# Rotary attention on one core: where a key projection, the tiles of context sums and the placing of queries stand around the shared bank

## What is computed

```python
xn = layer_norm(x, gamma_x, beta_x)
ln = layer_norm(latents, gamma_l, beta_l)
q = (ln @ Wq).reshape(b, m, h, d)
kv_x = xn @ Wkv
kv_l = ln @ Wkv
...
k_x = rope_rotate_k(k_x)
...
sim = jnp.einsum('bhid,bhjd->bhij', q, k)
attn = jax.nn.softmax(sim, axis=-1)
out = jnp.einsum('bhij,bhjd->bhid', attn, v)
out = jnp.transpose(out, (0, 2, 1, 3)).reshape(b, m, INNER)
return out @ Wo
```

## Time and profile before

| what | value |
|---|---|
| median of 3 runs | 2913.48 us (2912.77 to 2924.5) |
| the profiled execution: its own time, its span | 2919.26 us, 2917.5 us |
| PE busy over the span | 2579.3 us, 88% |
| DVE, ACT, POOL busy over the span | 61%, 56%, 48% |
| the 64 steps of the stage | 1984.5 to 2706.6 us |

### The profile page before, as it was taken

One profiled execution on the slowest core, in us unless ns is written; L12 is line 12 of the kernel. 1 busy time (PEld: TensorE's weight loads), 2 busy tenths in 40 slices (PEclk: granted clock), 3 DMA queues, 4 the chain that ended last, 5 costly groups with the idle time before them and its releaser, 6 DMA issues. The chain is left out here.

```text
span 2917.5 us, 43850 instructions
## 1 busy us (share of the span) xinstructions
PE 2579.3 (88%) x16307; PEld 2153.6 (74%) x16307; DVE 1791.1 (61%) x3679; ACT 1629.2 (56%) x2848; POOL 1407.9 (48%) x1114
## 2 busy tenths in 40 slices
PE   5999998587999999999958695878999999999777
PEld 4899988376999999999957564775676676767546
DVE  7888874545555555555445445338888888888352
ACT  4888884334766666666623243325666666666322
POOL 1877774111766666666600260206566665664040
PEclk9999999788999999999978897888999999999875
DMA  3323321012010111111001240212000000000000
GB/s 108 100 73 104 104 58 36 14 30 86 24 46 24 41 29 37 33 35 35 12 7 43 71 113 16 59 22 62 17 24 13 24 20 17 24 13 1 25 1 15
DMA packets 222574, 117.83 MB, mean 40 GB/s; under 512 B 21368, under 2 KB 217632, under 8 KB 222368
## 3 DMA queue, kind: packets, MB, share of 16 engines
q1 hardware_dynamic: 222368, 115.11, 14.3%
HBM read 100.39 MB, written 13.64 MB: 39 GB/s over the span
## 5 line engine op out<-in xcount | busy, mean ns | idle before, releaser
L812 POOL TENSOR_TENSOR L_xattn_held<-L_xattn_held,L_xattn_shift 128x512 f32<-128x512 f32 (+1 forms) x613 | 763.0, 1289 | 298.4 <-ACT L_xattn_shift L732 298.4
L532 PEld LDWEIGHTS L_xattn_acc<-L_xattn_rows,L_xattn_held 128*128 128x128 f32 (+2 forms) x5120 | 619.7, 192 | 34.3 <-DVE L_xattn_mixed L915 8.7
L532 PE MATMUL L_xattn_acc<-L_xattn_rows,L_xattn_held 128*128 128x129 f32 (+2 forms) x5120 | 629.1, 276 | 5.2 <-DVE L_xattn_mixed L915 5.2
L936 DVE TENSOR_TENSOR L_xattn_running<-L_xattn_ring,L_xattn_running 128x512 f32<-128x512 f32 (+1 forms) x384 | 264.1, 688 | 270.3 <-PE L_xattn_ring L514 258.8
L1566 POOL TENSOR_TENSOR L_xattn_projected<-L_xattn_along,L_xattn_crossed 128x512 f32<-128x512 f32 (+1 forms) x256 | 271.9, 1073 | 280.8 <-DVE L_xattn_crossed L1633 278.7
L722 ACT ACTIVATE L_xattn_held<-L_xattn_held 128x512 f32<-128x512 f32 (+2 forms) x640 | 400.3, 631 | 0.2
L715 ACT COPY L_xattn_held<-L_xattn_ring 128x512 f32<-128x512 f32 (+1 forms) x416 | 243.3, 585 | 227.6 <-DVE L_xattn_running L936 193.1
L512 PE MATMUL L_xattn_ring<-L_xattn_queries_hi,L_xattn_keys_hi 128*128 128x512 f32 (+2 forms) x640 | 282.5, 441 | 3.4 <-DVE L_xattn_keys_lo L840 2.0
L514 PE MATMUL L_xattn_ring<-L_xattn_queries_hi,L_xattn_keys_lo 128*128 128x512 f32 (+2 forms) x640 | 254.4, 397 | 0.0
L513 PE MATMUL L_xattn_ring<-L_xattn_queries_lo,L_xattn_keys_hi 128*128 128x512 f32 (+2 forms) x640 | 253.8, 397 | 0.0
L1282 PE MATMUL L_xattn_sums<-L_xattn_probT,L_xattn_rows 128*128 128x256 f32 (+2 forms) x896 | 248.9, 385 | 0.6 <-ACT L_xattn_mixed L1458 0.6
(11 more groups left out here) (576 smaller groups left out, 4872.2 us busy)
## 6 DMA issues: line engine op xcount, KB each, us to landing
L_xattn_raw<-in_ctx SPq DMA_DIRECT2D x16, 768.0 KB
context_normalised<-L_xattn_fresh SPq DMA_DIRECT2D x16, 768.0 KB
L_xattn_rows<-context_normalised SPq DMA_DIRECT2D x16, 768.0 KB
L_xattn_fresh<-in_ctx SPq DMA_DIRECT2D x16, 768.0 KB
L_xattn_rows<-in_ctx SPq DMA_DIRECT2D x16, 768.0 KB
L_xattn_staged<-in_ctx SPq DMA_DIRECT2D x16, 768.0 KB
L_xattn_xhat<-context_normalised SPq DMA_DIRECT2D x16, 768.0 KB
L_ffn_w<-in_L_ffn_W SPq DMA_DIRECT2D x2, 896.0 KB, 5.3
```

The lines of the kernel that those rows point to most:

```text
L532: mm = nc.tensor.matmul(acc[:, c // 2, c % 2 * WIDE:(c % 2 + 1) * WIDE], held[0:n, u % 2, k, c * P:(c + 1) * P], rows[0:n, b % 2, k, :], s ...
L812: nc.gpsimd.tensor_tensor(tile, tile, shift[0:keys_of_tile[k]], ALU.subtract).then_inc(shifted, 1)
L936: seen = nc.vector.tensor_tensor(most, bank, most, ALU.max)
```

## The change

Three things move, and nothing is added or left out. On PE, in the quad that follows another use of `bank_a` (j - 1 in `BETWEEN[t]`), the projection of the chunk is issued ahead of the transposes instead of behind them. The tiles of sums are spread by a new table `SPLIT` (tiles ahead of the other use, tiles behind it): in steps 1 and 2, quad 1 keeps one on either side, and quad 2 has both ahead of the second transfer and none behind it. On ACT, `keep_queries` is cut in two: `take_queries` stays where it was, and `place_queries` with `keep_own` comes after the evacuation of the next quad.

```diff
@@ -1058,7 +1058,10 @@
-    PIECES = [[range(0, 2), range(2, 4), range(4, 6), range(6, 7)], [range(7, 9), range(9, 11), range(11, 13), range(13, KT)]]
+
+    HALF = KT // 2
+    SPLIT = {0: ((2, 0), (1, 1), (2, 0), (1, 0)), 1: ((2, 0), (1, 1), (2, 0), (1, 0)),
+             2: ((2, 0), (1, 1), (2, 0), (1, 0)), 3: ((2, 0), (2, 0), (1, 1), (1, 0))}
...
@@ -1268,20 +1271,20 @@
-            def sum_context(pair, parity, group, part, piece, turned, tiles=slice(None)):
+            def sum_context(pair, parity, group, tiles, turned):
 
                 b = pair * 2 + parity
-                if part == 0 and piece == 0 and tiles.start is None:
+                if tiles.start == 0:
                     pe.wait_ge(a_free, turned)
...
-                for k in PIECES[part][piece][tiles]:
+                for k in tiles:
                     n = tile_of_keys[k][1]
...
-                if part == 1 and piece == len(PIECES[1]) - 1 and tiles.start is None:
+                if tiles.stop == KT:
                     mm.then_inc(sums_done, 1)
...
@@ -1300,17 +1303,21 @@
                     turns, projects = not (first and t == 0), not (last and t == R - 1)
                     scores(pair, parity, t, first and t == 0)
                     back, group, part = sums_of_slot(t)
+                    tile = part * HALF
                     for j in range(len(QUADS)):
+                        sums, between = not (first and back), BETWEEN[t].get(j)
+                        ahead, behind = SPLIT[t][j]
+
+                        if projects and j - 1 in BETWEEN[t]:
+                            project(*following(pair, parity, t), j)
                         if turns:
                             turn_probs(*preceding(pair, parity, t), j)
-                        if projects:
+                        if projects and j - 1 not in BETWEEN[t]:
                             project(*following(pair, parity, t), j)
                         if first and t == 0 and j < len(LATE):
                             late(j)
-                        sums, between = not (first and back), BETWEEN[t].get(j)
-
                         if sums:
-                            sum_context(*(before if back else (pair, parity)), group, part, j, turned, slice(None, 1))
+                            sum_context(*(before if back else (pair, parity)), group, range(tile, tile + ahead), turned)
                         if between == "queries":
...
-                        if sums:
-                            sum_context(*(before if back else (pair, parity)), group, part, j, turned, slice(1, None))
+                        if sums and behind:
+                            sum_context(*(before if back else (pair, parity)), group, range(tile + ahead, tile + ahead + behind), turned)
+                        tile += ahead + behind
...
@@ -1418,9 +1425,11 @@
-            def keep_queries(pair):
-
+            def take_queries():
                 emptied(nc.scalar.copy(asked[:], take()[:]))
+
+            def place_queries(pair):
+
                 act.drain()
...
@@ -1472,6 +1481,10 @@
                     for j in range(len(QUADS)):
                         if turns:
                             keep_probs(preceding(pair, parity, t)[2], j)
+                        if BETWEEN[t].get(j - 1) == "queries" and not last:
+                            if parity == 1:
+                                place_queries(pair + 1)
+                            keep_own(*after)
                         if j == 0:
                             exps(pair, parity, t)
                         if first and t == 0 and j < len(LATE):
@@ -1479,9 +1492,7 @@
                         between = BETWEEN[t].get(j)
                         if between == "queries":
                             if parity == 1 and not last:
-                                keep_queries(pair + 1)
-                            if not last:
-                                keep_own(*after)
+                                take_queries()

```

More of the change, by code:

```diff
@@ L1379, in _ @@
                 back, group, part = sums_of_slot(t)
-                for piece in range(4):
-                    sum_context(LAST, 1, group, part, piece, turned)
+                sum_context(LAST, 1, group, range(part * HALF, (part + 1) * HALF), turned)
             output(LAST)
@@ L1519, in _ @@
             keep_own(0, 0)
-            keep_queries(0)
+            take_queries()
+            place_queries(0)
             keep_rows(0, 0)
```

## The result

The changed kernel takes 2888.26 us (median of 4 runs, 2885.62 to 2892.13), the kernel before 2917.41 us (4 runs); the ratio is 0.9899 with a 95% interval of 0.9872 to 0.9926. Measured anew on two other occasions it is 0.9910 (0.9895 to 0.9925) and 0.9913 (0.9900 to 0.9926), where the kernel before is at 2915.31 and 2913.41 us. So the change is worth 26 to 29 us by these medians.

A forecast was written before the change was run, and what follows sets the result against it. PE was taken as the bound. Gains of 8.7 (steps 1 and 2), 4.9 (queries), 0.7 (output) and 0.6 us (batch 0) made 14.9, taken as 14.5: from 2913.5 to 2899 us, range 2890 to 2911.

The forecast's parts named there:

- Step 0 with queries: 7 places: the 1.12 us wait becomes about 0.9 before the next step's first turned quad, for ACT's division; gain 0.7 us.
- Steps 1 and 2: Batches 1 to 14: the first transfer's stall goes, the second's stays in step 1; gains 0.28 and 0.34 us per step.
- The junction: Tile of sums behind the last quad's transposes: if it pays 0.05 us, 28 times, the gain is 13.1 us.
- Step 3 and step 0 without queries: Step 3 with output gains 0.1 us, 7 times; step 0 without queries counted unchanged, its reordering covered by POOL's 0.42 us.
- Batch 0: No sums in its steps 1 and 2, so the projection stands under the wait; estimated gain 0.6 us for both.
- the projection would wait for DVE: Rival, 4%: quad 2's earlier projection waits for its bank, 0.5 us lost in each of 28 steps; 2923 us.
- More goes than I count: Rival, 13%: bank returned sooner or maximum earlier, so step 1 gains 0.3 and step 2 0.15 us more; 2891 us.

The follow-up runs named there:

- e5: The changed kernel with step 1's tile of sums behind the first transfer moved behind the second; batches 1 to 14 take 617.9 us, ratio to before 0.9908.
- e2: The kernel before with only the projection moved ahead of the turned quad behind another bank use; batches 1 to 14 take 636.7 us, ratio 0.9961.
- e6: The changed kernel with the four placing copies moved to step 3 of the same batch; batches 1 to 14 take 614.9 us, ratio to before 0.9898.
- e4: The changed kernel without its ACT part, queries placed at once as before; batches 1 to 14 take 632.6 us, ratio to before 0.9952.
- e3: The kernel before with only the new spread of tiles of sums (`SPLIT`); batches 1 to 14 take 651.8 us, ratio 1.0030.
- e8: e4 with one tile of sums in step 0 moved from quad 0 to quad 2; batches 1 to 14 take 627.5 us, ratio to before 0.9934.

## Why the prediction was wrong

What bounds the stage, where each stall goes, and the sign were right. The size was not: 14.5 us for about 26. What failed is the sum of the stalls: in the 14 batches it has 14.3 us and the traces have 19.9. Of the 5.6 us between them 3.1 lie in the steps with queries and those behind them, 0.9 in the other steps 1, 0.8 in the steps 2 and 0.8 in the steps 3 with output.

- **Step 0 with queries.** This term was mis-sized most. I had 0.7 for the step and the usual 0.28 for the one behind it; measured are 1.42 together. The wait moved to the division as forecast. Up to there 0.85 was gained (9.01 to 8.16); my own times give 2230.4 less 2222.16, 8.24, which I had rounded up to 8.3. From that quad to the first transfer it is 3.61 us (2215.30 to 2218.91) where it was 3.76, so 0.15 more, as the transfer no longer waits for an evacuation queued behind exponentials that waited for the maximum. I had named that in the rival of a larger gain and left it out of the sum. The other 0.42 came from the transfer to the next scores.
- **Steps 1 and 2.** Forecast 0.28 and 0.34, measured 0.41 and 0.40. The bank's gaps are 1.30 and 1.36 us for my 1.33 to 1.39. I took the projection behind a tile of sums at its full 0.77, as it is behind transposes; tile and projection take 1.13 together (2173.98 to 2175.11), for my 1.20.
- **The junction.** The Trainium skill (TensorE: Matmul & The Clock Gate, "Part 2: What happens when you issue a matmul") says that weight loads are pulled ahead of matmuls in flight, so that the next tile's load runs under this one's matmul; that this would hide them whatever stands before was my reading of it. The traces here do not bear that out for short transposes: behind the four of a quad a projection starts after 0.36 us and has 0.31 for its first matmul in place of 0.23, and a tile of sums starts after 0.44 in place of 0.36, so about 0.08 is exposed in either order. At the last quad, the place that I had named, part of it did come up: the tile of sums starts 0.27 after the transposes do, where the projection started after 0.19, and takes 0.44 in place of 0.48 to the scores. That is 0.71 where 0.19 and 0.48 make 0.67. But my sum had taken 0.70 there, so the loss to 13.1 us that I had weighed did not follow.
- **Step 3 and step 0 without queries.** Step 3 with output gave 0.22 for my 0.1. The 0.09 gained in step 3 without output and the 0.08 lost in the step 0 behind it belong together: 20.29 us in both before, 20.28 after, so that this pair is unchanged, as forecast. PE comes to the scores of that step 0 sooner, but they then wait longer for POOL; the second half of these scores in batch 4, before and after:

```profile
2172.18 1.35 PE L1256 MATMUL L_xattn_score<-L_xattn_projected,L_xattn_queries 128*128 128x512 f32 x4 [0.42 <-POOL L_xattn_projected L1566]
...
2158.16 1.35 PE L1259 MATMUL L_xattn_score<-L_xattn_projected,L_xattn_queries 128*128 128x512 f32 x4 [0.49 <-POOL L_xattn_projected L1578]
```

  From the first quad of the step to its last it is 6.00 us before (2173.36 to 2179.36) and 5.99 after (2159.34 to 2165.33): the two tiles of sums that now stand alone there cost nothing.
- **Batch 0.** Estimated at 0.6. From its first scores to those of batch 1 it took 47.9, 47.5 and 50.3 us in the traces before, 47.1, 46.0 and 45.3 after: 2.4 on the mean of three, from numbers that scatter as much as that.
- **What is left.** Medians differ by 26.2 to 29.2 us, of which 22.3 are accounted for. Without batch 0 and the 14 batches the traces have 2229.5, 2221.8 and 2214.0 us before, 2217.2, 2221.1 and 2219.0 after. These overlap, and on the mean of three they are 2.7 us apart. So 4 to 7 us on the medians stay open: neither shown to be the change's nor to be scatter. The stage alone, 22.3 of 2913.5 us, gives a ratio of 0.9923, which lies at the upper end of all three intervals, but inside each.
- **The rivals.** That the projection would wait for DVE did not happen: its only wait in the stage is 0.4 us of issue. "More goes than I count" was the nearest, 2891, and part of its mechanism came true: the exponentials behind the queries start sooner.

With the 22.3 us of the stage the forecast would have been 2891, on the edge of the range that I gave and still 3 above the median. So it takes the low sum and the open rest together to leave the range, which was too narrow for a sum of many small terms, nearly all of them sized low.

## What to carry to other kernels

A single shared bank has a price from fill to fill (1.30 to 1.36 us here: fill, evacuation and two hand-overs); spread the other work so that the starts of any two fills are at least that far apart, and take it from where they are further apart than that (e5). Moving work ahead of a wait lengthens the wait: in e2 the longer one came with a lower clock that took back 6.8 of 10.3 us, so look at what follows the wait too. A long copy on an engine that works its list off in order belongs where that engine is idle anyway, not merely one place later (e6). Judge a change of under one per cent on the stretch of the trace that repeats, and add up its side effects on the next step, not only the stall that it removes.

## What was unexpected of the hardware

After 1.56 us in which PE stood still, the scores behind took 4.50 us in place of 2.80 in 7 of 14 places (4 in e2, 3 in e4), with a granted clock of 0.63 over one such stretch. After 1.12 us in the three traces of the kernel before and in e3, and 1.13 in e8, they did so in none of 35. Whole executions of one and the same kernel differ by up to 19 us, by several us in stages that no edit touches (the first stage: 499.7 to 508.6 us over 14 traces).
